# Layer 3's attention: v's first chunk a half batch later, x's statistics a batch earlier, the division behind the norm

## The chip, the cores and the metric

The kernel runs on one core of one Trainium2 chip. The metric is the device time of one execution in microseconds; three runs of the kernel before gave 2774.33, 2770.84 and 2770.33 us, with a median of 2770.84 us. TensorE's granted clock averages 0.98 of full speed over the profiled execution.

## The reference, cut to what matters

Four layers run one after the other on x (16 batches, 112 rows, 256 columns, float32). Each layer is a gated cross attention to a context of 375 rows and then a gated feed-forward net. In layer 3 the attention is, for each batch:

```python
xn = (x - mean(x)) / sqrt(var(x) + 1e-5)
q = xn @ Wq.T + bq ; k = ctx @ Wk.T + bk ; v = ctx @ Wv.T + bv
s = split_heads(q) @ split_heads(k).T * 0.25       # 16 heads of 16
s = s + mask * -1e15
x = x + tanh(g_xattn[3]) * (merge_heads(softmax(s) @ split_heads(v)) @ Wo.T + bo)
```

The change touches only where, in the order of each engine's work, some of these steps stand.

## The kernel before, in words

`attention_stage` is built once for each layer; layer 3 has 16 heads of 16 (`hd == 16`), `mask="scores"`, and is `divided`: the probabilities are used unnormalized and the result is divided afterwards. Every engine has its own queue, written out batch by batch by `batches` (L223) for t = -1 to 16. A body of t is four **cycles** (i = 0 to 3, `NG`), each for four heads. In a cycle TensorE (L843) does, in this order: the scores of the next group of four heads (`scores`, L807), the product with v of the group before (`pv`, L838), and then three times a `turn` (L820, four transposes of probabilities into PSUM), with the **uses** of the table `CYCLES[3]` (L242 to L245) between them. A use is one job of projection work for a neighbouring batch: `k` (L712), `v` (L720), `xT` (L727, two transposes of the normalized x), `q` (L735), `rt` (L748), `out` (L753). The entries of a cycle's row are the positions 0 to 3: position 0 stands ahead of turn 0, position p behind turn p - 1. `k`, `v`, `xT` and `q` work on batch t + 1 (`LAG`, L253).

Turns and uses share three PSUM banks (`BANKS`, L247) in strict rotation: places are counted through the table, and ("rest",) takes a place without work, so that the count of a body is a multiple of three (L292). Before a use or turn TensorE waits until what was last on its bank has been copied out (`bank_free`, L693). ScalarE copies turn 0 and k, v, xT, q and rt; VectorE copies turns 1 and 2 (`copy_turn`, L1170).

VectorE's body (L1307) is, in cycle 0: `row_max` of the next four heads (L1146, reads the scores from PSUM and writes masked scores and the maximum), `divide_o` of batch t - 1 (L1181, needs the last `pv` and `rt`), `begin_norm` of batch t + 1 (L1064 to L1068: statistics, aggregate, add epsilon), the copy of turn 1, `norm_apply` of batch t + 1 (L1075, writes xn, for which `xT` waits), the copy of turn 2. `begin_norm` ends in a signal for GpSimd, whose `power` (L572) takes the root; `norm_apply` waits for it. Layer 3 issues it at i == 0 for t + 1 (`normed = 1`, L302; L1322), the other layers at i == 2 for t + 2. In cycle 2 VectorE has `halve_q` (L1134), in cycle 3 `invert` (L1158) and, at the end, `row_stats` of batch t - 1 (L1193).

ScalarE's body (L1013) is in each cycle: the exponentials of heads 0 and 1 (L931), the copy of turn 0 (L938), the copies of position 1, the exponentials of heads 2 and 3, the copies of positions 2 and 3. GpSimd's body (L660) is `power(t + 1)`, a memset of v's buffers in the first two bodies (L664), `add_bias(t + 1)` (L578, waits for xn), a root for the norm of the next net (L188), `spread(t)` (L613), and in the body of t = -1 `add_bias(0)` and `clear_spent` (L128), which clears the semaphores of a stage that is over.

Of the kernel before, what the change touches and what calls it, by code (L numbers as in the profile page):

```python
# [51 lines left out]
def exists(b):  # L52

    return not isinstance(b, int) or 0 <= b < B
# [168 lines left out]
def batches(eng, body, tail):  # L223

    for b in range(-1, B + tail):
# [13 lines left out]
        [[("rest",)], [("q", 0)], [("out",)], []],  # L239
        [[("rest",)], [("k", 1)], [("v", 0, 0)], []],  # L240
        [[], [("v", 1, 0)], [("v", 2, 0)], [("rt",)]]],
    3: [[[], [("k", 0)], [("v", 0, 0)], [("xT",)]],  # L242
        [[], [("out",)], [("q", 0)], []],
        [[], [("v", 1, 0)], [], []],
        [[], [("k", 1)], [("v", 2, 0)], [("rt",)]]],  # L245
}
BANKS, TURNS = 3, 3  # L247
# [16 lines left out]
def attention_stage(core, layer, heads, hd, scale, rope=False, mask=None, kan=False, moe=None):  # L264
# [13 lines left out]
    NG = heads // GH  # L278
# [3 lines left out]
    divided = late and not kan  # L282
# [16 lines left out]

    copies_last = layer == 2  # L300

    normed = 1 if layer == 3 else 2  # L302
    by_scalar = 2 if copies_last else 0
    by_vector = [k for k in range(TURNS) if k != by_scalar]
    kv = [j for j in jobs if j[0] in ("k", "v")]
# [9 lines left out]
    with ExitStack() as ctx:  # L315
# [56 lines left out]
        xT = sb("xT", [P, DC, S])  # L372
# [3 lines left out]
        v = sb("v", [KT, 2, KC, heads, VW])  # L376
# [158 lines left out]
        with nc.Block() as block:  # L535
# [30 lines left out]
            def _(pool):  # L566
# [3 lines left out]
                def power(b):  # L570
                    pool.wait_ge(s_ln.sem, s_ln.at(b, 2))
                    pool.tensor_tensor(rstd[:], rstd[:], core.minus_half[:], ALU.pow).then_inc(s_pow.sem, 1)  # L572

                def add_bias(b):

                    pool.wait_ge(s_xn.sem, s_xn.at(b))
                    pool.sem_inc(s_tick[3].sem, 1)
                    pool.tensor_tensor(x_all[:, b, :], x_all[:, b, :], borow[:], ALU.add).then_inc(s_biased.sem, 1)  # L578
# [75 lines left out]
                def net_rows(b):  # L654
                    norm_net.root(pool, b, b)
                    if rows_by_gpsimd:
                        pool.wait_ge(norm_net.s_root.sem, b + 1)
                        norm_net.apply(pool, b, b)

                def body(t, par):  # L660
                    if layer == 3 and exists(t + 1):
                        power(t + 1)
                    if hd == 16 and isinstance(t, int) and t < 1:
                        pool.memset(v[:, t + 1], 0.0).then_inc(s_zero.sem, 1)  # L664
                    if rope and exists(t + 1):
                        rope_add(t + 1, 1 - par, 0)
                    if exists(t) and exists(t + 1):
                        add_bias(t + 1)
                    if rope and exists(t + 1):
                        rope_q(t + 1)  # L670
                    if early(t - 2):
                        net_rows(t - 2)
                    if exists(t + 2) and layer != 3:
                        power(t + 2)
                    if divided and exists(t):
                        spread(t)
                    if rope and exists(t + 1):
                        rope_add(t + 1, 1 - par, 1)
                    if isinstance(t, int) and t == -1:
                        pool.wait_ge(s_bo.sem, 3 if late else 1)  # L680
                        add_bias(0)
                        core.clear_spent(pool)

                if layer != 3:
                    power(0)
                batches(pool, kan_body if kan else body, tail)

            @block.tensor
# [353 lines left out]
            def _(dve):  # L1042
# [35 lines left out]
                def make_mask(b, par):  # L1078
                    in_ctx(dve, b, par, s_maskin)
                    if has(b, 2):  # L1080
                        dve.wait_ge(s_max.sem, s_max.at(b - 2, heads - 1))

                    dve.tensor_scalar(mask_add[:, par, :], mask_in[:, par, :], 1.0, FLT_MAX, ALU.subtract, ALU.mult)\
                        .then_inc(s_mask.sem, 1)
# [90 lines left out]
                def divide_o(b):  # L1175
                    dve.wait_ge(s_pv.sem, s_pv.at(b, NG - 1))
                    dve.wait_ge(s_rtc.sem, s_rtc.at(b))
                    if has(b, 1):

                        dve.wait_ge(s_out.sem, s_out.at(b - 1))  # L1180
                    dve.tensor_tensor(oT[:], o_ps[:, 0:OC * S].rearrange("p (c s) -> p c s", c=OC), rt[:], ALU.mult)\  # L1181
                        .then_inc(s_o.sem, 1)
# [8 lines left out]
                def row_stats(b):  # L1191
                    hold(s_x.sem, s_x.at(b))
                    dve.bn_stats(core.row_stats[:, b, :], x_all[:, b, :]).then_inc(s_stats.sem, 1)  # L1193
# [54 lines left out]
                def copies(t, par, i, pos):  # L1248
                    for u in uses_at(t, i, pos):
                        copy_use(u, t, par)  # L1250
# [51 lines left out]
                def begin_norm(b):  # L1302
                    if moe:
                        dve.wait_ge(moe.x_in[b], 16)
                    norm_stats(b)

                def body(t, par):  # L1307
                    for i in range(NG):
                        groups = ahead(t, par, i)
                        for group in groups:  # L1310
                            row_max(*group)
                        if copies_last and exists(t):
                            copy_turn(t, i, by_vector[0])
                        if layer == 2 and i == 0 and exists(t + 1):
                            norm_apply(t + 1)
                        if i == 0 and divided and exists(t - 1):
                            divide_o(t - 1)
                        if divided and i == NG - 1 and exists(t):
                            invert(t, par)
                        if hd == 16 and i == 2 and exists(t + 1):  # L1320
                            halve_q(t + 1, 1 - par)
                        if i == (0 if layer == 3 else 2) and exists(t + normed):  # L1322
                            begin_norm(t + normed)
                        copies(t, par, i, 1)
                        if exists(t):
                            copy_turn(t, i, 1)
                        if rope and exists(t + 1):
                            if ("k", 0) in cycles[i][1]:
                                partners_k(t + 1, 0)
                            if ("k", 1) in cycles[i][1]:  # L1330
                                partners_k(t + 1, 1)
                            if ("q", 0) in cycles[i][1]:
                                partners_q(t + 1)
                        if i == 0 and exists(t + 1):
                            if layer != 2:
                                norm_apply(t + 1)
                            if mask == "keys":
                                make_mask(t + 1, 1 - par)
                        copies(t, par, i, 2)
                        if not copies_last and exists(t):  # L1340
                            copy_turn(t, i, 2)
                        copies(t, par, i, 3)
                        if divided and isinstance(t, int) and t == -1 and i == 1:
                            value_bias()
                        if mask == "scores" and isinstance(t, int) and t == -1 and i == 1:
                            dve.wait_ge(s_maskin[0].sem, 16)
                            dve.tensor_scalar(mask_add[:, 0, :], mask_in[:, 0, :], -1e15, None, ALU.mult)\
                                .then_inc(s_mask.sem, 1)
                            dve.wait_ge(s_mask.sem, 1)
                        if not late and isinstance(t, int) and t == -1 and i == 0:  # L1350
                            dve.tensor_scalar(borow[:], borow[:], gate, None, ALU.mult).then_inc(s_bo.sem, 1)
                            dve.memset(probs[:], 0.0).then_inc(s_zero.sem, 1)
                        if not late:
                            for group in groups:
                                scale_probs(*group)
                        if i == 1 and early(t - 2):
                            net_settle(t - 2)
                        if i == 2 and early(t - 2) and not rows_by_gpsimd:
                            norm_net.apply(dve, t - 2, t - 2)
                        if i == NG - 1 and exists(t - 1):  # L1360
                            row_stats(t - 1)

                def kan_setup():
                    dve.wait_ge(s_tail.sem, 16 * len(tail_weights))
# [9 lines left out]
                if kan:  # L1374
                    norm_stats(0)
                    norm_apply(0)
                elif layer != 3:
                    begin_norm(0)
                batches(dve, kan_body if kan else body, tail)

# [1209 lines left out]
```

## Time and profile before

| | |
|---|---|
| median of 3 runs | 2770.84 us (2770.33 to 2774.33) |
| profiled execution: time, span | 2773.1 us, 2771.3 us |
| TensorE busy over the span | 2625.3 us, 95% |
| VectorE, ScalarE, GpSimd busy | 1544.7, 1301.0, 643.8 us |
| layer 3's attention: start of its first matmul, of its first and last norm | 2096.50, 2098.2, 2397.6 us |

Times are counted from the start of the span. A timeline's line gives its start, its duration from first start to last end, the engine, the line of the kernel, the operation with output and inputs, how many records it merges, and in brackets the idle time of the engine before it with what ended it. Matmuls are pipelined, so that the distance from one start to the next says more than a duration.

### The profile page before, as it was taken

How to read it: one execution, taken by the hardware profiler on the slowest of the kernel's cores; microseconds unless marked ns; L12 is line 12 of the kernel's file. 1: busy time of each engine (PE TensorE's matmuls, PEld its weight loads, DVE VectorE, ACT ScalarE, POOL GpSimd, SP SyncE). 2: the span in 40 equal slices, each digit the busy share in tenths (PEclk: the TensorE clock that was granted, in tenths of full speed). 3: DMA queues.
4: the chain of work that ended last, by engine and by line, in shares of the span. 5: the costliest groups of instructions: out<-in, count | busy, mean ns of one | idle time of the engine just before them, and what ended most of it. 6: DMA issues, size and time to landing. Idle time of an engine off the chain costs nothing. (4 is left out here: it accounts for less than half of the span.)

```text
span 2771.3 us, 56714 instructions
## 1 busy us (share of the span) xinstructions
PE 2625.3 (95%) x19818; PEld 1983.4 (72%) x19818; DVE 1544.7 (56%) x4177; ACT 1301.0 (47%) x3610; POOL 643.8 (23%) x626
## 2 busy tenths in 40 slices
PE   6999978999999999989899998999998999979998
PEld 4777755666666666656666666999996777768887
DVE  4778746555555555536777774333325777842222
ACT  4777733343334434421566663333335777732222
POOL 1666661000000000000444431222221111113332
PEclk9999989999999999989999998999999999999999
DMA  4000002000000000010000006999992000059896
GB/s 124 18 18 18 12 16 94 13 13 7 13 7 13 7 13 7 1 34 1 21 18 20 22 7 219 330 325 332 326 328 58 24 18 24 7 197 311 304 313 224
DMA packets 91811, 267.57 MB, mean 97 GB/s; under 512 B 25068, under 2 KB 50804, under 8 KB 77268
## 3 DMA queue, kind: packets, MB, share of 16 engines
q1 hardware_dynamic: 74356, 242.53, 25.3%
q0 software_dynamic: 13632, 18.62, 3.1%
q10 hardware_dynamic: 3616, 3.67, 0.4%
q8 instruction: 128, 2.10, 0.3%
q14 instruction: 79, 0.65, 0.1%
HBM read 248.13 MB, written 16.65 MB: 96 GB/s over the span
## 5 line engine op out<-in xcount | busy, mean ns | idle before, releaser
L820 PEld LDWEIGHTS a_full_ps<-ident,a_probs 112*125 112x125 f32 x2688 | 367.0, 189 | 129.7 <-issue 64.5
L1917 PEld LDWEIGHTS m_banks<-m_x_inT,m_w 128*128 128x128 f32 x3824 | 435.1, 192 | 15.2 <-issue 13.5
L1917 PE MATMUL m_banks<-m_x_inT,m_w 128*128 128x128 f32 x3824 | 442.2, 276 | 1.4 <-ACT m_x_inT L1988 0.9
L931 ACT ACTIVATE a_probs<-a_masked,a_negmax 112x375 f32<-112x375 f32 x512 | 305.4, 598 | 287.7 <-DVE a_negmax L1146 287.7
L820 PE MATMUL a_full_ps<-ident,a_probs 112*125 112x112 f32 x2688 | 417.3, 281 | 18.3 <-ACT a_pT L938 5.6
L1172 DVE COPY a_pT<-a_full_ps 125x448 f32<-125x448 f32 x448 | 277.5, 621 | 222.1 <-PE a_full_ps L820 217.2
L720 PE MATMUL a_full_ps<-attention_room 128*125 128x256 f32 (+1 forms) x960 | 331.1, 474 | 9.8 <-ACT a_qT L921 3.9
L712 PE MATMUL a_full_ps<-attention_room 128*128 128x375 f32 x896 | 324.0, 490 | 13.8 <-PEq L1760 8.6
L1146 DVE CUSTOM_DVE_ANT_0 a_masked<-a_sc_ps,a_mask_add 112x375 f32<-112x375 f32 x512 | 249.8, 545 | 33.2 <-PE a_sc_ps L807 32.0
L931 ACT ACTIVATE a_probs<-a_sc_ps,a_negmax 112x375 f32<-112x375 f32 x384 | 217.0, 577 | 91.1 <-DVE a_negmax L1152 91.1
L838 PEld LDWEIGHTS a_o_ps<-a_pT,a_v 125*32 125x32 f32 (+1 forms) x5376 | 164.5, 118 | 126.5 <-issue 98.1
L807 PE MATMUL a_sc_ps<-a_kT,a_qT 32*112 32x375 f32 (+1 forms) x1792 | 241.7, 514 | 7.2 <-ACT a_probs L931 3.8
L1928 PE MATMUL m_banks<-m_w,m_hid 128*128 128x256 f32 x992 | 232.9, 383 | 0.0
L720 PEld LDWEIGHTS a_full_ps<-attention_room 128*125 128x125 f32 x960 | 165.9, 189 | 89.8 <-issue 65.6
L838 PE MATMUL a_o_ps<-a_pT,a_v 125*32 125x112 f32 (+1 forms) x5376 | 216.3, 265 | 6.3 <-DVE a_pT L1172 2.6
L712 PEld LDWEIGHTS a_full_ps<-attention_room 128*128 128x128 f32 x896 | 159.8, 194 | 84.9 <-issue 15.5
L1152 DVE TENSOR_REDUCE a_negmax<-a_sc_ps 112x2 f32<-112x750 f32 x192 | 171.2, 933 | 79.1 <-PE a_sc_ps L807 79.1
L2002 ACT ACTIVATE m_silu<-m_banks,m_b 128x128 f32<-128x128 f32 x280 | 102.7, 368 | 239.4 <-PE m_banks L1917 231.7
L1928 PEld LDWEIGHTS m_banks<-m_w,m_hid 128*128 128x128 f32 x992 | 179.9, 190 | 32.0 <-issue 11.9
L2146 DVE SCALAR_TENSOR_TENSOR m_hid<-m_banks,m_b,m_silu 128x128 f32<-128x128 f32 x280 | 98.0, 351 | 157.8 <-ACT m_silu L2002 157.8
L2002 ACT ACTIVATE m_silu<-m_banks 128x128 f32<-128x128 f32 x216 | 59.6, 276 | 213.0 <-PE m_banks L1917 213.0
L938 ACT ACTIVATE a_pT<-a_full_ps 125x448 f32<-125x448 f32 x224 | 120.0, 536 | 62.6 <-PE a_full_ps L820 61.1
(253 smaller groups left out, 3451.8 us busy)
## 6 DMA issues: line engine op xcount, KB each, us to landing
m_w<-in_L2f_w SPq DMA_DIRECT2D x105, 1024.0 KB, 6.8
m_w<-in_L3f_w SPq DMA_DIRECT2D x72, 768.0 KB, 4.8
attention_room<-in_ctxT SPq DMA_DIRECT2D x64, 375.0 KB, 3.1
m_w<-in_L3f_w SPq DMA_DIRECT2D x36, 640.0 KB, 5.6
m_b<-in_L2f_b SPq DMA_DIRECT2D x35, 128.0 KB, 7.9
p_rows<-normed SPq DMA_DIRECT2D x16, 224.0 KB, 6.3
attention_room<-in_L0x_spline_wT SPq DMA_DIRECT2D x1, 2048.0 KB, 10.3
net_room<-in_L1f_w SPq DMA_DIRECT2D x2, 1024.0 KB
```

Of the source, the lines that this page charges most:

```text
L712: mm = pe.matmul(use_ps[:, 0:SK], wk[:, c, u[1] * P:(u[1] + 1) * P], ctxT[:, par, c, :], start=(c == 0), stop=(c == DC - 1))
L720: mm = pe.matmul(use_ps[0:KT, 0:v_width], ctxT[:, par, c, k * KT:(k + 1) * KT], wv[:, c, part * v_width:(part + 1) * v_width], start=(c == ...
L807: pe.matmul(sc_ps[:, a, 0:SK], lhs, kT[r:r + k, par, c, :], start=True, stop=True)\
L820: mm = pe.transpose(full_ps[0:KT, bank_of["turn", i, k], (j % 4) * S:(j % 4 + 1) * S], probs[:, i % 2, a, t * KT:(t + 1) * KT], ident[0:S, ...
L838: mm = pe.matmul(o_ps[a % WIDE * VW:(a % WIDE + 1) * VW, block * S:(block + 1) * S], v[:, par, t, head(i, a), :], pT[:, i % 2, KC * a + t, :],
L931: act.activation(probs[:, i % 2, a, 0:SK], src, ACT.Exp, bias=negmax[:, m:m + 1], scale=-1.0 if mask else 1.0, accum_out=rowsum[:, par, n: ...
L1146: dve.tensor_tensor_reduce(out=masked[:, i % 2, a, :], in0=sc_ps[:, a, 0:SK], in1=bias, scale=-1.0, scalar=FLT_MAX, op0=ALU.add, op1=ALU.m ...
L1152: dve.tensor_reduce(negmax[:, m:m + 2], sc_ps[:, 2 * a:2 * a + 2, 0:SK], AX.X, ALU.max, negate=True).then_inc(s_max.sem, 1)
L1172: dve.tensor_copy(pT[:, i % 2, 4 * k:4 * (k + 1), :], full_ps[0:KT, bank_of["turn", i, k], 0:4 * S] .rearrange("p (j s) -> p j s", j=4)).t ...
L1917: mm = pe.matmul(ab_ps[:, (par * FC + f) % RING, i * SLOTS:(i + 1) * SLOTS], w[:, par, c, f * P:(f + 1) * P], x_inT[:, c, :], start=(c == ...
L1928: mm = pe.matmul(y_ps[:, par, 0:D], hid[parts[f], f, :], w2[parts[f], par, f, :], start=(f == 0), stop=(f == FC - 1))
L2002: act.activation(silu[parts[f], i, :], ab_ps[0:r, i, 0:SLOTS], ACT.Silu, bias=b1[0:r, par, f:f + 1] if biased else 0.0).then_inc(s_silu.se ...
```

## The change

It gives `CYCLES[3]` another table: v's first chunk leaves position 2 of cycle 0 and stands in position 1 of cycle 2, v's second chunk moves there from position 1 to position 2, and three rests are added, so that 24 places rotate instead of 21. `begin_norm` for batch t + 2 becomes the last thing of VectorE's cycle 3, behind `row_stats`, and the first one runs ahead of the bodies; `divide_o` moves behind `norm_apply` in cycle 0; GpSimd's `power(t + 2)` stands at the end of its body; and `clear_spent` moves, in layers 1, 2 and 3, from the body of t = -1 to the end of the body of t = 0.

```diff
-    3: [[[], [("k", 0)], [("v", 0, 0)], [("xT",)]],
-        [[], [("out",)], [("q", 0)], []],
-        [[], [("v", 1, 0)], [], []],
+    3: [[[], [("k", 0)], [], [("rest",), ("xT",)]],
+        [[("rest",)], [("out",)], [("q", 0)], []],
+        [[], [("v", 0, 0)], [("v", 1, 0)], [("rest",)]],
         [[], [("k", 1)], [("v", 2, 0)], [("rt",)]]],
...
-    normed = 1 if layer == 3 else 2
+    normed = 2 if layer != 3 else 2
+
+    stats_last = layer == 3
...
                 def body(t, par):
-                    if layer == 3 and exists(t + 1):
-                        power(t + 1)
...
-                    if exists(t + 2) and layer != 3:
+                    if exists(t + 2) and not stats_last:
                         power(t + 2)
...
                         pool.wait_ge(s_bo.sem, 3 if late else 1)
                         add_bias(0)
+                    if exists(t + 2) and stats_last:
+                        power(t + 2)
+                    if isinstance(t, int) and t == 0:
                         core.clear_spent(pool)
-                if layer != 3:
-                    power(0)
+                power(0)
...
-                        if i == 0 and divided and exists(t - 1):
+                        if i == 0 and divided and not stats_last and exists(t - 1):
                             divide_o(t - 1)
...
-                        if i == (0 if layer == 3 else 2) and exists(t + normed):
+                        if not stats_last and i == 2 and exists(t + normed):
                             begin_norm(t + normed)
...
+                        if i == 0 and stats_last and exists(t - 1):
+                            divide_o(t - 1)
                         copies(t, par, i, 2)
...
                             row_stats(t - 1)
+                        if stats_last and i == NG - 1 and exists(t + 2):
+                            begin_norm(t + 2)
...
-                elif layer != 3:
+                else:
                     begin_norm(0)
```

## Rows read from the trace of the kernel before

**Rows 1.** Windows view: us; busy of PE, PEld, DVE, ACT, POOL; clock; DMA share; GB/s.

```profile
2210.00:2311.00 101.00, 99.84 (x1060) 73.69 (x1060) 80.14 (x265) 73.51 (x226) 11.11 (x20) 1.00 0.07 21
```

**Rows 2.** Timeline, TensorE, the end of a cycle 3 and the cycle 0 behind it.

```profile
2230.24 0.59 PE L820 MATMUL a_full_ps<-ident,a_probs 112*125 112x112 f32 x4
...
2230.66 0.35 PE L748 MATMUL a_full_ps<-ident,a_rexp 112*128 112x112 f32 x2
...
2230.95 0.90 PE L807 MATMUL a_sc_ps<-a_kT,a_qT 32*112 32x375 f32 x8
...
2234.30 0.59 PE L820 MATMUL a_full_ps<-ident,a_probs 112*125 112x112 f32 x4
...
2234.72 1.04 PE L720 MATMUL a_full_ps<-attention_room 128*125 128x256 f32 x4
...
2235.60 0.59 PE L820 MATMUL a_full_ps<-ident,a_probs 112*125 112x112 f32 x4
...
2236.36 0.39 PE L727 MATMUL a_full_ps<-ident,a_xn 112*128 112x112 f32 x2 [0.18 <-DVE a_xn L1075]
...
2236.68 0.90 PE L807 MATMUL a_sc_ps<-a_kT,a_qT 32*112 32x375 f32 x8
```

**Rows 3.** Waits view of the stretch 2200 to 2300: us, times, longest us.

```profile
PE a_full_ps L727 <- DVE a_xn L1075: 0.9, 5, 0.2
```

**Rows 4.** Timeline, VectorE, from turn 2 of cycle 3 through cycle 0.

```profile
2230.86 0.62 DVE L1172 COPY a_pT<-a_full_ps 125x448 f32<-125x448 f32 x1 [0.68 <-PE a_full_ps L820]
...
2231.41 0.42 DVE L1193 BATCH_NORM_STATS2 row_stats<-x_all 112x6 f32<-112x256 f32 x1
...
2232.02 0.55 DVE L1146 CUSTOM_DVE_ANT_0 a_masked<-a_sc_ps,a_mask_add 112x375 f32<-112x375 f32 x1 [0.19 <-PE a_sc_ps L807]
...
2233.90 0.39 DVE L1181 TENSOR_TENSOR a_oT<-a_o_ps,a_rt 128x224 f32<-128x224 f32 x1
...
2234.20 0.42 DVE L1064 BATCH_NORM_STATS2 a_stats<-x_all 112x6 f32<-112x256 f32 x1
...
2235.05 0.61 DVE L1172 COPY a_pT<-a_full_ps 125x448 f32<-125x448 f32 x1
...
2235.80 0.41 DVE L1075 TENSOR_SCALAR a_xn<-x_all,a_mv,a_rstd 112x256 f32<-112x256 f32 x1
```

**Rows 5.** Timeline, TensorE and ScalarE, the end of a cycle 1 and cycle 2.

```profile
2220.90 0.60 PE L820 MATMUL a_full_ps<-ident,a_probs 112*125 112x112 f32 x4
...
2221.43 0.90 PE L807 MATMUL a_sc_ps<-a_kT,a_qT 32*112 32x375 f32 x8
...
2223.55 1.04 PE L720 MATMUL a_full_ps<-attention_room 128*125 128x256 f32 x4
...
2224.29 0.52 ACT L938 ACTIVATE a_pT<-a_full_ps 125x448 f32<-125x448 f32 x1
...
2224.43 1.19 PE L820 MATMUL a_full_ps<-ident,a_probs 112*125 112x112 f32 x8
...
2225.54 0.90 PE L807 MATMUL a_sc_ps<-a_kT,a_qT 32*112 32x375 f32 x8
```

**Rows 6.** Timeline, the norm and xT of batch 0 and of batch 1.

```profile
2098.17 1.45 DVE L1075 TENSOR_SCALAR a_xn<-x_all,a_mv,a_rstd 112x256 f32<-112x256 f32 x1 [0.69 <-POOL a_rstd L572]
...
2100.68 0.36 PE L727 MATMUL a_full_ps<-ident,a_xn 112*128 112x112 f32 x2
...
2113.87 1.22 DVE L1075 TENSOR_SCALAR a_xn<-x_all,a_mv,a_rstd 112x256 f32<-112x256 f32 x1
...
2115.24 0.38 PE L727 MATMUL a_full_ps<-ident,a_xn 112*128 112x112 f32 x2 [0.64 <-DVE a_xn L1075]
```

**Rows 7.** Timeline, GpSimd: its addition in layer 3, behind a batch's norm.

```profile
2236.39 0.72 POOL L578 TENSOR_TENSOR x_all<-x_all,attention_room 112x256 f32<-112x256 f32 x1 [0.63 <-DVE a_xn L1075]
```

**Rows 8.** Timeline, GpSimd in layer 2, behind `clear_spent` and ahead of a later body.

```profile
1336.29 1.38 POOL L664 MEMSET a_v<- 125x1536 f32 x1 [0.30 <-issue]
...
1361.06 0.85 POOL L585 TENSOR_TENSOR a_rot_a<-a_k_raw,attention_room 128x375 f32<-128x375 f32 x1 [3.43 <-ACT a_k_raw L892]
```

## The prediction

> **What bounds the kernel now.** I read the windows by stage first. In the steady part of layer 3's attention TensorE is busy 99.84 of 101.00 us at a granted clock of 1.00, while VectorE has 80 and ScalarE 74 [rows 1]. So time can be won only where TensorE waits, and any new wait costs its whole length. I then read TensorE's timeline by distances from start to start, which show waits that the modelled ends blur. I call s the start of a cycle's scores. Cycle 0 begins at 2230.95 and the next scores are at 2236.68: 5.73 us [rows 2]. A turn takes 0.42 us when nothing is in its way (2230.24 to 2230.66, ahead of `rt`), but from turn 2 of cycle 0 to `xT` it is 0.76 us (2235.60 to 2236.36): 0.34 us of waiting in each batch [rows 2]. The waits view puts it down to xn from VectorE, 0.9 us in 5 batches [rows 3]; it counts from the modelled end and so sees half of it. All of it, 15 times 0.34, is 5 us.
>
> VectorE's timeline tells why xn is late [rows 4]. In cycle 0 it masks four heads (from s + 1.07 to s + 2.95), divides, takes the statistics, and copies turn 1 only at s + 4.10; the norm follows at s + 4.85 and `xT` 0.56 us behind its start.
>
> **What the change removes.** In cycle 0 v's first chunk no longer stands between turn 1 and turn 2: 0.88 us of TensorE (2234.72 to 2235.60) [rows 2], and a copy on ScalarE. The division and the statistics leave the front of VectorE's queue, and the norm no longer waits for GpSimd's root.
>
> **What still orders cycle 0.** The norm (L1336) stands behind the copy of turn 1 (L1326) in VectorE's program, and turn 1 comes behind k as before. So the norm cannot be had when TensorE wants it:
> - turn 1 starts at s + 3.35 (2234.30) [rows 2]; nothing ahead of it changes;
> - a copy starts 0.62 us after its turn when it waits only for that (2230.24 to 2230.86) [rows 2, 4]: s + 3.97. Before, it was at 4.10, behind the statistics;
> - the next VectorE instruction starts 0.55 us behind the start of a copy (2230.86 to 2231.41) [rows 4]: norm at s + 4.52;
> - `xT` 0.56 us behind the norm (2235.80 to 2236.36) [rows 2, 4]: s + 5.08;
> - the next scores 0.32 us later [rows 2]: s + 5.40.
>
> Cycle 0 becomes 5.40 instead of 5.73 us: **-0.33**. TensorE gives up 0.88 us of work there and mostly waits instead: turn 2 could start at 3.77 and `xT` at 4.19.
>
> **Is VectorE free at s + 3.97?** `begin_norm` now runs ahead of the masks. `row_stats` starts at s + 0.46 (2231.41) [rows 4]. The next statistics I start 0.30 to 0.42 us later (0.30 is what lies between the division and the statistics, 0.42 the duration of `row_stats`), and they take 0.85 us until the next instruction (2234.20 to 2235.05). The masks then begin at s + 1.6 to 1.75 instead of 1.07 and end 1.88 us later (2232.02 to 2233.90) [rows 4], at 3.5 to 3.65, ahead of 3.97. Exponentials move back by 0.6 us with them; the first of them is wanted only by turn 0 of the next cycle, and ScalarE has lost v's copy. The division now starts at s + 4.94, the copy of turn 2 0.30 us later at 5.24, as before (2236.22 would be 5.27), over at 5.86; the next `pv` needs it, and comes behind scores that run from 5.40 to 6.30.
>
> **Cycle 2 pays for v.** Before, it takes 4.11 us (2221.43 to 2225.54) [rows 5]: v's chunk at s + 2.12, turn 1 at 3.00, and then turns 1 and 2 back to back, 1.11 us to the next scores. Afterwards, from turn 1: turn to v 0.42 (2234.30 to 2234.72), v to turn 2 0.88 [rows 2], turn 2 to scores 0.53 (2220.90 to 2221.43) [rows 5], together 1.83. The added v lands on the bank of turn 0, which ScalarE copies until s + 3.38 (2224.29 plus 0.52) [rows 5]; a release takes up to 0.15 us (xn ends at 2236.21, `xT` starts at 2236.36), which holds it from 3.42 to at most 3.53; its weight load is what is released, so I take 3.46. So cycle 2 ends at 3.46 + 0.88 + 0.53 = 4.87: **+0.76**. It is less than v's 0.88 because the two bare turns took longer than 0.42 + 0.53. Its copy adds 0.37 us to a ScalarE that has room. Bounds: 0.71 if the bank is free at once, 0.88 if nothing is won.
>
> In cycles 1 and 3 work and order stay. The rotated banks put `out` behind `xT`'s copy and turn 1 of cycle 1 behind the copy of turn 2, both over before they are wanted.
>
> **The sum.** 14 bodies (t = 1 to 14) have both a cycle 0 with `xT` and a cycle 2 with v: 14 x (0.76 - 0.33) = +6.0 us. Body 0: its norm takes 1.22 us instead of 0.41, since GpSimd's memset runs beside it; the memset moves ahead of it, so `xT` starts at 2113.87 + 0.56 = 2114.43 instead of 2115.24: -0.8, and cycle 2 +0.76. Start: `xT` of batch 0 waits for v's chunk until 2100.68 and could start at 2098.17 + 1.45 + 0.15 = 2099.77: -0.9, v filling a wait for q later [rows 6]. Bound: 0 if something else holds q. The last batches have no v or `xT`: 0. Together **+5.0 us**.
>
> One rule bears on the memset. Its row shows the norm at three times its length [rows 6]. The Trainium skill ("SBUF — State Buffer", the section on the two sides) says that VectorE's two-port operations and GpSimd exclude each other from a shared pair of ports for a whole instruction; the row agrees in kind. By that rule the new first norm still collides, as I take it.
>
> **`clear_spent`** moves in three layers. In layer 2, 0.30 us of issue lie between the addition and the memset behind it; at its new place GpSimd waits 3.43 us in a later body anyway [rows 8]. I take 0; uncovered it would cost 0.3 us in a layer, 0.9 in all. Roots and additions on GpSimd stay covered as long as it idles for most of a batch (busy 11 of 101 us) [rows 1]. No DMA moves: the last v, which releases a context buffer, keeps its place, and so does the first k, which waits for one.
>
> The profiled execution took 2773.1 us, 2.3 above the median of the three runs. It becomes 2778.1; the median 2775.8 (+0.18%).
>
> **The rivals.**
> 1. **xT is free** (slower becomes faster). If xn were ready when TensorE has done turn 2, cycle 0 would be 3.77 + 0.42 + 0.32 = 4.51, -1.22 a batch. With +0.76 and the one-off gains: 14 x -0.46 - 0.95 = -7.4 us, 2763.4. For it: VectorE loses 1.15 us ahead of the copy (2233.90 to 2235.05) [rows 4]. Against: the copy then waits for turn 1 itself. It decides if the norm starts before s + 3.77; then the gain passes 0.2%. 8%.
> 2. **The statistics block the masks.** If `begin_norm` takes so long that the masks end at s + 4.3, cycle 0 wins nothing and v costs its 0.76: 14 x 0.76 - 0.95 = +9.7, 2780.5. For it: a wait for the statistics of an earlier instruction lies between each two. Against: rows 4 time the same chain at 0.85 us. 14%.
> 3. **GpSimd's addition holds the division back.** It starts 0.59 us after the norm and takes 0.72 [rows 7], and now meets the division rather than a copy from PSUM. Pushed back by its whole length, the copy behind the division would end at 6.58 and `pv` start at 6.7 instead of 6.3: 14 x 0.4 more, 2781.4. Against: the division starts 0.42 us behind the norm, before it. 4%. The Trainium skill's rule above, in the same section, locks only for two SBUF inputs or two-port operations; the division reads PSUM once, so the rule gives no cost.
> 4. **The start brings nothing**: +5.9, 2776.7. I hold it within the forecast.
>
> **How the numbers follow.** The forecast has 72%, with 2773.5 to 2778.5 as its own range (0.10 us a batch in the chain, 0.9 at the start, 1 us of spread in the runs). About 0.2%, 5.5 us, is what a measurement of this kernel can tell from no change; the forecast lies just inside, so 43 of its points go to "same" and 29 to "slower". With rivals 2 and 3 slower has 0.47, same with the rest 0.45, faster 0.08. The range is 2771.5 to 2780.6: it holds the forecast and rival 2, and leaves out rivals 1 and 3.
>
> **What the profile would show.** Right: `xT` waiting some 0.6 us or more for xn in each batch, cycle 0 at 5.40, cycle 2 at 4.87 and cycles 1 and 3 at 4.94 and 5.41, a batch at 20.62 instead of 20.19 us; the copy of turn 1 waiting for TensorE; masks in cycle 0 0.6 us later. Wrong: cycle 0 near 4.5 us, the norm ahead of s + 3.8, or a wait in cycle 1 or 3.

## The result: slower by 0.2%, and the profile after

| | before | after |
|---|---|---|
| runs, median | 10 runs, 2774.07 us (2770.33 to 2775.34) | 10 runs, 2779.41 us (2777.72 to 2781.25) |
| ratio, 95% interval | | 1.0024 (1.0016 to 1.0032) |
| profiled execution: time, span | 2773.1, 2771.3 us | 2778.16, 2776.3 us |
| layer 3's attention, first k to first transposition of the next net ("the stage") | 336.56 us | 343.43 us |
| its start: first k to the scores that open body 0 | 12.61 us | 13.36 us |
| body 0; median of bodies 1 to 14, and their sum | 20.90; 20.19; 282.97 us | 20.91; 20.64; 289.38 us |
| cycles 0, 1, 2, 3 (medians) | 5.73, 4.94, 4.11, 5.41 us | 5.38, 4.94, 4.92, 5.41 us |
| from the last body's first scores to the end of the stage | 20.08 us | 19.78 us |

The two medians lie 5.34 us apart, which is 0.19%; the ratio above is taken over all the runs and not as the quotient of the two medians. The stage is 6.87 us longer in the profiles: 0.75 at the start, 0.01 in body 0, 6.41 in 14 batches, -0.30 at the end. The spans differ by only 5.0 us, because in this pair of executions the stage began 1.77 us earlier. Most of that, 1.6 us, is there in TensorE's timeline behind the end of layer 0's attention already, which no part of the change touches (first of before, then of after). The same operation started at 410.63 us in a second profile of before, and between 407.6 and 412.4 in the variants of after told of below. Counted over all ten runs the time rose by 4.4 to 8.9 us (the interval of the ratio), which holds the stage's 6.87.

```profile
410.57 3.70 PE L1475 MATMUL f_w_ps<-net_room 128*128 128x255 f32 x16 [1.42 <-PEq L535]
```

```profile
408.97 3.69 PE L1481 MATMUL f_w_ps<-net_room 128*128 128x255 f32 x16 [1.42 <-PEq L537]
```

TensorE's and VectorE's lines of the attention are 2 higher in the kernel after (L727 became L729, L1075 L1077), those of the nets 6 (L1475 became L1481). The windows view of after, same stretch as [rows 1]: TensorE is busy 1.4 us less and every other engine has done less in the same time.

```profile
2210.00:2311.00 101.00, 98.44 (x1042) 72.43 (x1044) 78.05 (x257) 70.68 (x220) 10.71 (x19) 1.00 0.07 21
```

The waits view of after, 2200 to 2300 us. The first is new, the second answers to [rows 3].

```profile
PE a_full_ps L822 <- ACT a_pT L940: 1.2, 5, 0.2
PE a_full_ps L729 <- DVE a_xn L1077: 1.1, 5, 0.2
```

TensorE's timeline of after in a cycle 0, as [rows 2], from s = 2232.22:

```profile
2232.22 0.90 PE L809 MATMUL a_sc_ps<-a_kT,a_qT 32*112 32x375 f32 x8
...
2234.29 1.44 PE L714 MATMUL a_full_ps<-attention_room 128*128 128x375 f32 x4
2235.57 0.59 PE L822 MATMUL a_full_ps<-ident,a_probs 112*125 112x112 f32 x4
2236.40 0.66 PE L822 MATMUL a_full_ps<-ident,a_probs 112*125 112x112 f32 x4 [0.24 <-ACT a_pT L940]
2237.29 0.38 PE L729 MATMUL a_full_ps<-ident,a_xn 112*128 112x112 f32 x2 [0.23 <-DVE a_xn L1077]
2237.60 0.90 PE L809 MATMUL a_sc_ps<-a_kT,a_qT 32*112 32x375 f32 x8
```

Turn 1 stands at s + 3.35 as before, turn 2 at 4.18, `xT` at 5.07, the next scores at 5.38. Turn 2 does not come at 3.77, where the prediction had it: it waits for ScalarE's copy of turn 0, which stands behind the late exponentials. The wait for xn that is left behind it is 0.47 us (5.07 less 4.18 and 0.42). VectorE's timeline of the same cycle, as [rows 4]:

```profile
2233.02 0.41 DVE L1066 BATCH_NORM_STATS2 a_stats<-x_all 112x6 f32<-112x256 f32 x1
...
2233.95 0.55 DVE L1148 CUSTOM_DVE_ANT_0 a_masked<-a_sc_ps,a_mask_add 112x375 f32<-112x375 f32 x1
...
2236.20 0.62 DVE L1174 COPY a_pT<-a_full_ps 125x448 f32<-125x448 f32 x1 [0.29 <-PE a_full_ps L822]
2236.74 0.40 DVE L1077 TENSOR_SCALAR a_xn<-x_all,a_mv,a_rstd 112x256 f32<-112x256 f32 x1
2237.06 0.38 DVE L1183 TENSOR_TENSOR a_oT<-a_o_ps,a_rt 128x224 f32<-128x224 f32 x1
```

The copy waits for turn 1 (s + 3.98), the norm follows (s + 4.52), the masks start at s + 1.73. GpSimd's addition [rows 7] starts 0.58 us behind the norm, when the division is under way; in layer 2 it runs straight into the memset now, without the 0.30 us of issue of [rows 8]:

```profile
2237.32 0.73 POOL L580 TENSOR_TENSOR x_all<-x_all,attention_room 112x256 f32<-112x256 f32 x1 [2.75 <-DVE a_xn L1077]
```

```profile
1333.74 0.64 POOL L580 TENSOR_TENSOR x_all<-x_all,attention_room 112x256 f32<-112x256 f32 x1
1334.32 1.38 POOL L664 MEMSET a_v<- 125x1536 f32 x1
```

And cycle 2, TensorE and ScalarE, as [rows 5], from s = 2221.90:

```profile
2221.90 0.90 PE L809 MATMUL a_sc_ps<-a_kT,a_qT 32*112 32x375 f32 x8
...
2224.02 1.04 PE L722 MATMUL a_full_ps<-attention_room 128*125 128x256 f32 x4
2224.89 0.59 PE L822 MATMUL a_full_ps<-ident,a_probs 112*125 112x112 f32 x4
2225.33 1.13 PE L722 MATMUL a_full_ps<-attention_room 128*125 128x256 f32 x4
2226.30 0.59 PE L822 MATMUL a_full_ps<-ident,a_probs 112*125 112x112 f32 x4
```

```profile
2224.76 0.52 ACT L940 ACTIVATE a_pT<-a_full_ps 125x448 f32<-125x448 f32 x1
```

The second chunk waits for the bank of turn 0, which ScalarE has copied at 2225.28, and starts 0.05 us later. Apart from the wait of turn 2, the batches run by the forecast's mechanism, within 0.05 us of its cycles. The start of the stage is not. TensorE's timeline of after there, against [rows 6]:

```profile
2094.73 2.84 PE L714 MATMUL a_full_ps<-attention_room 128*128 128x375 f32 x4 [8.56 <-PEq L1766]
2097.90 0.63 PE L729 MATMUL a_full_ps<-ident,a_xn 112*128 112x112 f32 x2 [0.34 <-DVE a_xn L1077]
2099.07 2.02 PE L737 MATMUL a_full_ps<-a_xT,attention_room 128*128 128x112 f32 x8 [0.54 <-ACT a_xT L905]
2100.89 1.74 PE L865 MATMUL a_o_ps<-attention_room,a_bvb 128*112 128x256 f32 x4
2102.47 1.89 PE L722 MATMUL a_full_ps<-attention_room 128*125 128x256 f32 x8
2104.94 0.90 PE L809 MATMUL a_sc_ps<-a_kT,a_qT 32*112 32x375 f32 x8 [0.58 <-DVE a_qT L1136]
```

The same stretch of before, which the prediction had read only up to `xT`:

```profile
2096.50 2.84 PE L712 MATMUL a_full_ps<-attention_room 128*128 128x375 f32 x4 [8.56 <-PEq L1760]
2099.13 1.72 PE L720 MATMUL a_full_ps<-attention_room 128*125 128x256 f32 x4
...
2101.66 1.12 PE L735 MATMUL a_full_ps<-a_xT,attention_room 128*128 128x112 f32 x8 [0.62 <-ACT a_xT L903]
2102.61 1.03 PE L863 MATMUL a_o_ps<-attention_room,a_bvb 128*112 128x256 f32 x4
2103.48 1.11 PE L720 MATMUL a_full_ps<-attention_room 128*125 128x256 f32 x4
2105.95 0.90 PE L807 MATMUL a_sc_ps<-a_kT,a_qT 32*112 32x375 f32 x8 [1.35 <-DVE a_qT L1134]
```

Counted from the first k, `xT` comes 1.01 us earlier (3.17 instead of 4.18), as forecast. But from there each step is slower: `xT` to q 1.17 instead of 0.98, q to the bias product 1.82 instead of 0.95, that to v 1.58 instead of 0.87; v to the first scores is 2.47 in both. The first scores come at 10.21 instead of 9.45. The windows view gives the clock. Of before, in steps of 2 us from its first k (seventh column, behind the five engines: granted clock):

```profile
2098.50:2100.50 2.00, 2.00 (x6) 1.43 (x5) 1.12 (x1) 0.57 (x1) 0.97 (x1) 0.50 1.11 268
2100.50:2102.50 2.00, 1.38 (x11) 1.12 (x10) 0.00 (x0) 0.63 (x2) 0.00 (x0) 0.99 0.83 142
```

Of after, the same:

```profile
2096.73:2098.73 2.00, 1.47 (x4) 0.29 (x2) 1.12 (x1) 0.73 (x2) 0.96 (x1) 0.50 1.11 293
2098.73:2100.73 2.00, 1.66 (x8) 1.69 (x9) 0.00 (x0) 0.20 (x1) 0.00 (x0) 0.50 0.74 125
2100.73:2102.73 2.00, 2.00 (x8) 1.59 (x8) 0.06 (x1) 0.60 (x2) 0.00 (x0) 0.60 0.11 9
```

In before TensorE had worked without a gap from k through v's chunk, and its clock was at the upper level (2.4 GHz) 4 us behind the first k. In after it stood twice, ahead of `xT` and of q, and was held at the lower level (1.2 GHz) over q and the bias product, until more than 7 us behind the first k. That was a reading; run 6 below tests it.

### The profile page after: what moved, and what is told of

The parts are those of the page before. It is cut to its first block and busy times, and to the rows that moved or that the text cites. A ratio compares the mean times of both kernels' runs of the same rounds, so it can differ in the third digit from the quotient of the medians.

```text
span 2776.3 us, 56714 instructions
## 1 busy us (share of the span) xinstructions
PE 2626.2 (95%) x19818; PEld 1983.4 (71%) x19818; DVE 1542.5 (56%) x4177; ACT 1296.4 (47%) x3610; POOL 642.9 (23%) x626
```

## The experiments

Each number below names a kernel; the passage set in is what was expected before it ran. Times of the stage are from its one profiled execution; where there are several runs, the ratio is given.

**1. The norm ahead of the copy of turn 1, in the kernel after.** My theory of the batches was that `xT` waits for a norm that stands behind the copy of turn 1; the rival, that the late masks hold it.

```diff
-                        if layer == 2 and i == 0 and exists(t + 1):
+                        if layer in (2, 3) and i == 0 and exists(t + 1):
                             norm_apply(t + 1)
...
-                            if layer != 2:
+                            if layer not in (2, 3):
                                 norm_apply(t + 1)
```

> The changed kernel, with the norm of the next batch ahead of the copy of turn 1 on VectorE in cycle 0. Theory 1 (xT waits because the norm stands behind that copy): the norm starts when the masks end, about 3.6 us into cycle 0; then turn 2 is the last to be ready, since its bank waits for ScalarE's copy of turn 0 until 4.15 us; xT at 4.6, cycle 0 4.9 instead of 5.38 us, a batch 20.17 instead of 20.65 us, the kernel some 6.7 us below the changed one. Theory 2 (the statistics ahead of the masks are the price): cycle 0 stays near 5.38, the time within 1 us of the changed kernel. Theory 0 (TensorE's own work is the price, no wait matters): no change.

Measured: cycle 0 5.00, `xT` at s + 4.68, a batch 20.26, stage 337.54; one run, 2773.73 us. The queue order was the wait for xn, which is gone. Turn 2 still starts at s + 4.18, held by ScalarE's copy of turn 0, and `xT` 0.49 us behind it; another wait lies at the same place, see 3.

**2. The statistics ahead of the masks, behind `invert`, in the kernel after.** This takes back the 0.66 us by which the masks had moved.

```diff
                             invert(t, par)
+                        if stats_last and i == NG - 1 and exists(t + 2):
+                            begin_norm(t + 2)
...
-                        if stats_last and i == NG - 1 and exists(t + 2):
-                            begin_norm(t + 2)
```

> The changed kernel, with begin_norm(t + 2) behind invert in cycle 3, where VectorE idles 0.83 us for turn 1, instead of at the cycle's end. The masks of cycle 0 start at 1.07 instead of 1.73 us. Theory 1: turn 2 starts earlier, xT does not: cycle 0 stays 5.38, a batch 20.65, the time as the changed kernel's within 1 us. Theory 2: cycle 0 shortens by 0.3 to 0.9 us, the time by 5 to 12 us.

Measured: masks back at s + 1.07, and cycle 0 still 5.38, a batch 20.64, stage 343.35; one run, 2778.33. In the new table with this order of the norm the late masks cost nothing: turn 2 now starts at s + 3.78 instead of 4.18, right behind turn 1, but `xT`, which comes behind it, waits for xn in both.

**3. Both.**

> The changed kernel with both edits: norm ahead of the copy of turn 1, statistics behind invert in cycle 3. Theory 1, with the bank of turn 0 as the next wait behind it: both waits are gone, turn 2 at 3.77, xT at 4.19, cycle 0 4.51 us, a batch 19.78 us; 14 x 0.87 = 12.2 us below the changed kernel, some 5.5 us below the kernel before (ratio to it 0.998). If cycle 0 is held by something else (TensorE's order of k and turns, ScalarE), it stays above 4.9 and the time within 1 us of the first of these runs.

Measured: cycle 0 5.00, `xT` at s + 4.65, a batch 20.26, stage 337.65; 10 runs, median 2774.07, ratio 1.0007 (0.9997 to 1.0016). The 4.51 did not come: there is a third wait, which I had not listed. TensorE and VectorE of this kernel, from s = 2228.56:

```profile
2233.21 0.41 PE L729 MATMUL a_full_ps<-ident,a_xn 112*128 112x112 f32 x2 [0.28 <-DVE a_pT L1174]
```

```profile
2231.51 0.41 DVE L1077 TENSOR_SCALAR a_xn<-x_all,a_mv,a_rstd 112x256 f32<-112x256 f32 x1
2232.53 0.62 DVE L1174 COPY a_pT<-a_full_ps 125x448 f32<-125x448 f32 x1 [0.61 <-PE a_full_ps L822]
```

xn is over at s + 3.36, and `xT` waits for the copy of turn 1 (s + 3.97 to 4.59), since the rest ahead of it puts it on turn 1's bank.

**4. The new table alone, on the kernel before.** `CYCLES[3]` as in the change, everything else as before.

> The kernel before with only the new table of cycles; VectorE's and GpSimd's orders as before. Theory 1: the norm stays at 4.85 us into cycle 0 behind division, statistics and the root, so cycle 0 stays 5.73 while cycle 2 grows to 4.92: a batch 21.00 instead of 20.19 us, 14 x 0.81 = 11.3, with body 0, start and tail about +12.5 us on the kernel before. If TensorE's work were all that counts (theory 0), moving v would cost nothing: a batch 20.19.

Measured: cycles 5.72, 4.94, 4.92, 5.41, a batch 20.99, stage 349.08, 12.5 more than before; one run, 2787.8. Its waits view, 2200 to 2300, against 0.9 in [rows 3]:

```profile
PE a_full_ps L727 <- DVE a_xn L1075: 5.2, 5, 1.0
```

This shows what the table does by itself: cycle 0 gains nothing from losing v's chunk, since the chunk lay inside the wait for xn, and cycle 2 pays for it. The start of its stage takes 13.37 us, as long as that of after (13.36), so the loss there comes with the table and not with the new orders; in run 5, which has the orders and the old table, it takes 12.64.

**5. The new order alone: the changed kernel with the old table.**

> The changed kernel with the old table: v's first chunk back in cycle 0, all orders of VectorE and GpSimd as changed. Theory 1: norm at 4.52, xT at 5.07 behind v and turn 2 at the same time (turn 2 starts at 4.65), cycle 0 5.39, cycle 2 4.11: a batch 19.85 instead of 20.19 us, 14 x 0.34 = 4.8 us and 0.8 us in body 0 below the kernel before (ratio 0.998). If the statistics ahead of the masks cost something by themselves, a batch is above 20.

Measured: cycles 5.77, 4.94, 4.12, 5.41, a batch 20.23, stage 336.01; 10 runs, median 2772.46, ratio 1.000 (0.999 to 1.001). The expected gain is missing, and `xT` no longer waits for xn. TensorE's timeline, then ScalarE's in cycle 0, from s = 2228.35:

```profile
2232.44 1.13 PE L722 MATMUL a_full_ps<-attention_room 128*125 128x256 f32 x4 [0.16 <-ACT a_pT L940]
2233.41 0.59 PE L822 MATMUL a_full_ps<-ident,a_probs 112*125 112x112 f32 x4
```

```profile
2231.87 0.52 ACT L940 ACTIVATE a_pT<-a_full_ps 125x448 f32<-125x448 f32 x1
```

The late masks make ScalarE's first exponentials late, its copy of turn 0 ends at 2232.39, and v, which in the old table needs that bank, starts at s + 4.09 instead of 3.77. So what the new table hides, the old one pays.

**6. A filler behind the first k, in the kernel after.** Where v's chunk stood in the start, TensorE multiplies the same operands again, into a PSUM tile that is written anew later; the result is unused.

```diff
                                 run_use(u, t, par)
+                                if layer == 3 and isinstance(t, int) and t == -1 and u == ("k", 0):
+                                    for c in range(DC):
+                                        pe.matmul(o_ps[0:KT, 0:D], ctxT[:, 1 - par, c, 0:KT], wv[:, c, 0:D],
+                                                  start=(c == 0), stop=(c == DC - 1))
```

> The changed kernel; in the body of t = -1 TensorE repeats v's first chunk into the idle o_ps bank right behind k, where v stood before; the result is not used. Theory clock (the start lost time because TensorE idled at the low clock and reached the high one only 7.6 us after its first matmul instead of 4.0): the granted clock is 1.00 again some 4 to 5 us after the first k, q takes 1.1 instead of 2.0 us, the first scores come 9.5 instead of 10.2 us after the first k. Rival (the new order of the start costs by itself, or x's way through ScalarE): the first scores come at 10.2 or later.

Measured: start 12.53 us (13.36 without), first scores 9.37 behind k, stage 342.54; one run, 2778.27. With more work the start is 0.83 us shorter. `xT` comes 4.19 us behind k, as in before, so this gives back what the clock cost and not what the earlier `xT` had won. Its windows from the first k at 2095.69, and its timeline:

```profile
2099.69:2101.69 2.00, 1.46 (x12) 1.20 (x11) 0.00 (x0) 0.36 (x1) 0.00 (x0) 0.99 0.79 137
```

```profile
2098.32 1.72 PE L858 MATMUL a_o_ps<-attention_room 128*125 128x256 f32 x4
2099.88 0.36 PE L729 MATMUL a_full_ps<-ident,a_xn 112*128 112x112 f32 x2
2100.77 1.12 PE L737 MATMUL a_full_ps<-a_xT,attention_room 128*128 128x112 f32 x8 [0.54 <-ACT a_xT L909]
```

The clock is up 4 us behind the first k as in before, and q and the bias product have their old lengths (1.12 and 1.03 us). With runs 4 and 5, which show that the loss comes and goes with the table, the cause of the longer start is shown. That a single run's time is not shorter than after's says nothing, since what lies ahead of the stage varies by more than 0.83 us.

**7. Matmuls ahead of the stage, in the kernel after.** 40 matmuls of the identity with itself at the end of layer 2's net, in TensorE's idle time, results unused (each leaves two records, x80 below).

> The changed kernel with 40 matmuls of the identity behind the last work of layer 2's net on TensorE, into a bank that nothing reads, so that TensorE is busy until the attention starts. Theory clock: the clock is 1.00 at the first k, k takes 1.4 instead of 2.8 us, q 1.1 instead of 2.0, the bias matmuls 1.0 instead of 1.7; x's norm now holds xT, and the first scores come 8.4 to 8.7 us after the first k instead of 10.2. Rival (it is not the clock): 10.2, and the matmuls only delay the stage.

Measured, not as the theory said: start 13.96, first scores 10.77, stage 344.11; one run, 2781.41. Its timeline and windows:

```profile
2086.67 9.09 PE L1948 MATMUL m_banks<-ident 128*128 128x128 f32 x80
2096.21 1.50 PE L714 MATMUL a_full_ps<-attention_room 128*128 128x375 f32 x4 [0.45 <-PEq L1766]
2099.39 0.63 PE L729 MATMUL a_full_ps<-ident,a_xn 112*128 112x112 f32 x2 [1.68 <-DVE a_xn L1077]
```

```profile
2098.21:2100.21 2.00, 0.63 (x2) 0.29 (x2) 1.13 (x1) 0.33 (x2) 0.98 (x1) 0.80 1.11 288
2100.21:2102.21 2.00, 1.65 (x8) 1.68 (x9) 0.00 (x0) 0.21 (x1) 0.00 (x0) 0.50 0.69 122
```

k did run at the upper level (1.50 us instead of 2.84), but that only made the wait for xn longer, 1.68 instead of 0.34 us, and around its end the clock fell, from 1.00 over the 2 us from k on to 0.80 and 0.50. A high clock won ahead of a wait was lost in the wait.

**8. The old table with the norm first and the statistics early** (the edits of 1 and 2, and `CYCLES[3]` of before).

> Norm ahead of the copy of turn 1, statistics behind invert, but v's first chunk in cycle 0 as before the change. Theory 1: xn is ready early, turn 2 starts at 4.65 behind v, xT at 5.07, cycle 0 5.39; cycle 2 4.11: a batch 19.85 us, 0.07 more than with the new table (whose cycle 2 has v between the two turns); with the earlier clock at the start the whole is within 1 us of the run that has both edits and the new table. If v between turn 1 and turn 2 covered something else too, this one is faster by several us.

Measured: cycles 5.36, 4.94, 4.11, 5.41, `xT` at s + 5.07, a batch 19.82, start 12.62, stage 330.59; 10 runs, median 2768.11 against 2772.52 of before, ratio 0.9983 (0.9973 to 0.9993). It beats both kernels. Against 5, the place of the statistics and of the norm is worth 0.41 us a batch. (`xT` is free here: turns, k and v alone fill the 5.36.)

**9 and 10. `xT` on another bank.** On the kernel of 3, `xT` and the rest ahead of it change places, so that it lies on the bank that ScalarE copied k from; the other kernel has the filler of 6 as well.

```diff
-    3: [[[], [("k", 0)], [], [("rest",), ("xT",)]],
+    3: [[[], [("k", 0)], [], [("xT",), ("rest",)]],
```

> The kernel with the norm ahead of the copy of turn 1 and the statistics ahead of the masks (cycle 0 5.00 us, xT at s + 4.65), with xT and the rest behind it exchanged in the last position of cycle 0: xT then lies on the bank that ScalarE copies k from, not on the one that VectorE copies turn 1 from. Theory (the copy of turn 1 is the third wait of xT): xT at s + 4.19, cycle 0 4.51, a batch 19.77 us, the stage 7 us shorter than with turn 1's bank (337.65), about 330.8. Rival (something else holds xT at 4.65, TensorE's own order or xn itself): cycle 0 stays at 5.00, a batch 20.26. Second rival: turn 0 of cycle 1, which now comes on xT's bank, waits for xT's copy; then cycle 0 is 4.51 and cycle 1 longer than 4.94.

Measured, without the filler: cycle 0 4.52, `xT` at s + 4.21, a batch 19.80; one run, 2765.78. That is the 4.51 that the prediction gave for a free `xT`. But the stage took 332.13, 1.3 more than expected, because its start took 14.61 us: `xT` of batch 0 now waits for the copy of k (0.73 us where it was 0.34), and the clock comes back later still. The windows from its first k at 2093.70:

```profile
2101.70:2103.70 2.00, 2.00 (x7) 1.54 (x6) 1.42 (x4) 0.00 (x0) 0.47 (x1) 0.50 0.00 0
2103.70:2105.70 2.00, 2.00 (x13) 1.20 (x11) 0.63 (x2) 0.83 (x3) 0.25 (x1) 0.75 0.01 4
```

> The same with the filler matmuls behind the first k of layer 3 (the work of one chunk of v, its result unused), which brought the start of the stage from 13.36 to 12.53 us. Theory: both gains add: start 12.5, a batch 19.77, stage about 330, a little shorter than with the old table, the norm first and the statistics early (330.59); time 2767 to 2768, 0.998 of the kernel before and about that of the best version so far. Rival (xT not free): batch 20.26, stage 336.8, time like before.

Measured, with the filler: start 12.55, a batch 19.80, stage 329.91; 8 runs, median 2764.76 against 2772.39, ratio 0.9973 (0.9963 to 0.9984). It is the fastest of the kernels here. Its stage is 6.65 us shorter than that of before, and its runs are 4.4 to 10.3 us faster (the interval of the ratio), which agrees. What the filler alone adds to the kernel's time is not measured: its stage is 2.2 us shorter than without, but the kernel without it had one run only, 2765.78.

**11. The clearing of the semaphores alone, and before again.**

```diff
                         add_bias(0)
-                        core.clear_spent(pool)
+                    if isinstance(t, int) and t == 0:
+                        core.clear_spent(pool)
```

> The kernel before with one part of the change alone: the clearing of spent semaphores moves in layers 1 to 3 from the body of t = -1 to the end of the body of t = 0. Theory (it costs and gains nothing): ratio 1.000, within 0.9990 and 1.0010, stage 336.6. Rival (0.3 us of issue in each layer leave the start of the stage, with GpSimd's memset and roots earlier behind them): up to 1.5 us shorter, 0.9995, with layer 3's attention beginning at 2095.

> The kernel before, unchanged, profiled a second time, for the spread of what lies ahead of the stage. In its first profile layer 3's attention began at 2096.50 us; in the changed kernel at 2094.73, and in nine variants between 2093.38 and 2097.39. Theory (that is spread between executions): the second profile puts it anywhere in 2093 to 2098, and the stage itself is 336.5 within 0.3. Rival (moving the clearing of the semaphores in layers 1 and 2 gains some 1.5 us ahead of the stage): it stays at 2096.5 within 0.5, and only the kernel with that edit is earlier.

Measured: the moved clearing, 11 runs, median 2772.55 against 2773.15, ratio 1.000 (0.9991 to 1.0009), stage 336.66, beginning at 2096.97. It costs and gains nothing. Before again: 2772.69, stage 336.55, a batch 20.19, beginning at 2096.12. So the stage repeats within 0.1 us. What lies ahead of it varies, though the kernels with the changed order lay mostly lower (2093.4 to 2096.5) than those with the old one (2096.1 to 2097.4); clearing is not why. Counted from the operation at 410 us shown above, layer 3's attention begins 1685.5 to 1686.6 us later in every profile but two (runs 1 and 5, 1683.2 and 1683.1), with or without the change. So most of this spread lies in layer 0, which no kernel here changes; where in it, and why it leans one way, stays open.

## Why the prediction was wrong

The time, 2779.41, lies inside the range and 3.6 us above the forecast of 2775.8. Of this, 3.2 us is the base: the forecast added its 5.0 us to a median of three runs, 2770.84, and ten runs of before gave 2774.07. The measured ratio of 1.0024 is above the 0.2% within which the forecast had put it; its interval reaches from 0.16% to 0.32% and so holds the forecast's 0.18%, and by the size of the rise alone the two can't be told apart. Between the profiled executions +5.0 us was forecast and +5.1 came (2773.1 to 2778.16). That agreement is luck: the stage gave +6.87, 1.87 more than forecast, and the stretch ahead of it, which the forecast left alone, -1.77.

- **The start: the step that failed.** The forecast said -0.9, with 0 as its bound on the worse side; +0.75 was measured. These 1.65 us are the largest part of the 1.87. The reasons given did hold: `xT` came 1.01 us earlier, and v's two chunks filled part of the wait that the first scores have for q (1.35 us of it before, 0.58 after). What the step left out is what the moved chunk had done for the clock. It had kept TensorE busy behind k, and without it the clock stayed at 1.2 GHz through `xT`, q and the bias product: +0.19 +0.87 +0.71, together 1.77. Run 4 shows the loss with the table alone, and run 6 gives it back with work of the same shape and no use. The bound of 0 was wrong too: taking work away ahead of a wait can lose on the clock. It could have been seen: at the start k and v take 2.84 and 1.72 us in before, where the same shapes take 1.44 (after's timeline above) and 1.04 [rows 2] in a batch.
- **The rule behind it.** The Trainium skill says, in "TensorE: Matmul & The Clock Gate", section on the HAM clock gate, that the clock gate follows how busy the engine has recently been, at 1.2 GHz when idle and at 2.4 when busy. The windows of before, after and runs 6, 7 and 10 agree in kind, but not in every part: in run 7 the clock stayed at the lower level for 6.8 us, of which TensorE was busy for 6.3. I had not weighed the rule, since [rows 1] show a clock of 1.00 for the batches.
- **Cycle 0**: 5.40 forecast, 5.38 measured, with copy, norm and `xT` at s + 3.98, 4.52 and 5.07 against 3.97, 4.52 and 5.08. Runs 1 and 4 show the mechanism from both sides: the new order under the new table shortens the cycle by 0.34, and the norm moved ahead by 0.38 more. Of the wait that was to show the forecast right, 0.6 us or more for xn, 0.47 was there, since turn 2 took 0.41 us of it.
- **Cycle 2**: 4.87 forecast, 4.92 measured. The second chunk started at s + 3.43, where 3.46 was taken, but its next turn came 0.97 us behind it and not 0.88: a chunk that has waited for its bank took 0.09 longer, as the same form did in run 5 (2232.44 to 2233.41). With cycle 0, a batch has +0.457 instead of +0.43: 0.4 us over 14 batches.
- **Body 0**: forecast -0.8 + 0.76, measured +0.01 in sum. The norm of batch 1 took 0.40 instead of 1.22 us, clear of the memset, while that of batch 0 still took 1.45 beside it.
- **The end**: 0 forecast, -0.30 measured. The last body has no v or `xT`, but its turns lie on other banks: its cycle 0 takes 4.11 instead of 3.18 us, cycle 1 4.37 instead of 4.85, and the stretch from the scores of cycle 2 to the product with v behind the next turns 4.24 instead of 4.99, where a wait of 0.81 us for ScalarE's copy is gone. I had taken all this as unchanged. The table does it: the stretch takes 19.77 to 19.79 us in all the kernels with the new table, run 4 with its old orders among them, and 20.07 or 20.08 in those with the old one. Which bank does what in it is not taken apart.
- **Masks, exponentials, division.** Masks moved by 0.66 us, 0.6 forecast, and cost nothing in this table, as forecast (run 2). But the reason given, that the first exponentials are wanted only by turn 0 of the next cycle, was wrong: ScalarE's copy of turn 0 stands behind them, and turn 2, or v in the old table, waits for that copy. The later norm hid it here, and in run 5 nothing did.
- **`clear_spent`**: 0 forecast, 0 measured (run 11).
- **The rivals.** 1 (`xT` free) did not come; what it lacked is now known: the norm ahead of the copy and a bank that is free, worth 0.38 and 0.46 us a batch (runs 1 and 10), besides the early statistics that run 10 has too; without them turn 2 starts at s + 4.18, which by itself rules out 4.51. Its cycle 0 of 4.51 was right, 4.52. Rival 2 is refuted by the masks, which end at s + 3.68 and not at 4.3, and by run 2; rival 3 by the division, which took 0.38 us beside the addition, and by cycle 1, which stayed at 4.94. Rival 4 was nearest and still too low, since the start lost time. The forecast lay 0.5 us inside the line of 0.2%; at such a distance each small term decides on which side a result falls, and here it was the least examined one.

## What to carry to other kernels

A piece of work that moves away should be priced three ways: by its length, by the wait that it covered (run 4), and by the clock that it kept up (run 6): at a start, durations of matmuls near twice those of the steady part give the last away. When a transfer or transpose waits, list all its conditions, its operand, its place in the queue and the bank that it lands on, since taking one away only shows the next (runs 1, 3 and 10). Filler work for TensorE shortened the start of a stage where it filled the wait (run 6, and 9 against 10) and lengthened it where it ended ahead of the wait (run 7); each of these is one profile.

## What the runs showed of the hardware

- In this start the clock cost more (1.77 us) than the earlier `xT` won (1.01). The same q (8 matmuls) took 1.12 us in before and in run 6 and 2.02 in after. The clock rose 4 us behind the first k where TensorE had worked through (before, 6, 9), 7.6 us with two gaps of 0.34 and 0.54 us (after), and 11 us with gaps of 0.73 and 0.54 (run 10).
- It fell again around the end of a wait of 1.68 us for xn, with 9 us of filler and k at the upper level just ahead of it (run 7), and then stayed low for 6.8 us, though TensorE was busy for 6.3 of them.
- A matmul group that had to wait for its bank took longer to the next start: v's chunk 0.97 us where 0.88 is usual (after and run 5), a turn 0.49 where 0.42 is usual (run 1).
- Beside GpSimd's memset of 1.37 us the norm of batch 0 took 1.45 us, in before and after; that of batch 1 took 1.22 beside a memset and 0.40 clear of it.
